# A graph network's adjacency stages: the gathered rows are weighed by ScalarE, tile by tile, in place of VectorE

## The reference, cut to what matters

```
h   = typed_linear(feat[src], W, etype)              # a message per edge
att = sigmoid(leaky_relu(h_l + h_r)) * edge_weight[:, None]
msg = h3.transpose(0, 2, 1) * att[:, None, :]
agg = segment_sum(msg, dst, num_segments=n_nodes)    # edges are sorted by dst
```

## Time and profile before

| | |
|---|---|
| device time, 3 runs | 4801.52 us median (4799.81 to 4803.82) |
| profiled execution | 4794.28 us, span 4792.6 us |
| busy: PE, DVE, ACT, POOL | 3187.0, 3208.5, 1384.8, 3339.1 us |
| mean granted PE clock | 0.827 |
| first stage, first to last gather | 197.8 to 2202.4 us |
| second stage, first to last gather | 2314.8 to 3304.0 us |

### The profile page before, as it was taken

How to read it: one execution, slowest core, us unless ns; L and a number is a source line. 1 busy time by engine, 2 the same in 40 slices (tenths; PEclk the granted TensorE clock), 3 DMA queues, 4 the chain that set the end, 5 groups by cost and what they waited for, 6 DMA issues and landing times. The chain is left out here.

```text
span 4792.6 us, 63834 instructions
## 1 busy us (share of the span) xinstructions
PE 3187.0 (66%) x16141; PEld 1906.6 (40%) x16141; DVE 3208.5 (67%) x5876; ACT 1384.8 (29%) x2465; POOL 3339.1 (70%) x3216
## 2 busy tenths in 40 slices
PE   2667777777777777775555555554678767487795
PEld 2344445445545544543343444443323232222222
DVE  4676776767776677775555555554588777487686
ACT  2422232323232323233322122222233222132352
POOL 0277777777777777773577777775777777777573
PEclk6798888988888898887777777776688879688897
DMA  1233332323332333232222222223356545255583
GB/s 52 98 94 93 94 98 85 102 85 100 92 99 89 96 94 96 90 98 85 91 80 71 65 78 71 71 71 102 89 157 172 149 120 153 75 166 155 159 245 108
DMA packets 355069, 502.09 MB, mean 105 GB/s; under 512 B 92892, under 2 KB 214749, under 8 KB 354574
## 3 DMA queue, kind: packets, MB, share of 16 engines
q1 hardware_dynamic: 251453, 394.51, 25.4%
q0 software_dynamic: 100352, 102.96, 10.1%
q10 hardware_dynamic: 2896, 0.59, 0.1%
HBM read 290.63 MB, written 207.16 MB: 104 GB/s over the span
## 5 line engine op out<-in xcount | busy, mean ns | idle before, releaser
L809 POOL DMA_INDIRECT frows<-messages,fidx x2352 | 2277.5, 968 | 848.5 <-issue 669.3
L889 PE MATMUL fps_b<-hot_key,hot_lo 128*128 128x343 f32 x3136 | 1233.8, 502 | 407.1 <-PEq L70 403.3
L948 DVE TENSOR_TENSOR strip<-strip,fps_b 128x343 f32 x1568 | 787.0, 502 | 541.7 <-DVEq L70 516.5
L1091 POOL DMA_INDIRECT lrows<-messages,lidx x784 | 879.2, 1121 | 271.2 <-issue 223.7
L879 PE MATMUL fps_sum<-hot,frows 128*64 128x80 f32 x4704 | 551.1, 301 | 601.9 <-PEq L70 601.9
L824 ACT ACTIVATE turned<-fps_t 128x512 f32<-128x512 f32 (+1 forms) x754 | 431.6, 572 | 1741.2 <-ACTq L70 1738.8
L889 PEld LDWEIGHTS fps_b<-hot_key,hot_lo 128*128 128x128 f32 x3136 | 541.6, 206 | 728.8 <-issue 679.1
L879 PEld LDWEIGHTS fps_sum<-hot,frows 128*64 128x64 f32 x4704 | 521.9, 194 | 693.0 <-issue 693.0
L918 DVE TENSOR_SCALAR hot_key<-iota_f,edge 128x343 f32<-128x343 f32 x1574 | 750.9, 477 | 0.1
L1236 ACT ACTIVATE pos<-l_c,coeff 128x896 f32<-128x896 f32 x392 | 394.6, 1007 | 725.2 <-PE l_c L1140 725.2
L1140 PE MATMUL l_c<-unit_t,unit_g 64*128 64x448 f32 x1568 | 460.9, 667 | 148.5 <-DVE acc L1278 89.1
(11 more groups left out here) (186 smaller groups left out, 1741.7 us busy)
## 6 DMA issues: line engine op xcount, KB each, us to landing
adj<-turned SPq DMA_DIRECT2D x696, 256.0 KB
edge<-adj SPq DMA_DIRECT2D x294, 448.0 KB
adj_x<-adj SPq DMA_DIRECT2D x98, 448.0 KB
frows<-messages,fidx POOLq DMA_INDIRECT x2352, 2.4
messages<-msg SPq DMA_DIRECT2D x14, 1120.0 KB, 4.6
lrows<-messages,lidx POOLq DMA_INDIRECT x784
adj<-turned SPq DMA_DIRECT2D x58, 64.0 KB
wh_g<-wh_rows SPq DMA_DIRECT2D x56, 32.0 KB, 1.7
```

The source lines that it names most:

```text
L809: pool.indirect_dma_start(rows[:, q, k, :], None, tab_l[l].ap(), bass.IndirectOffsetOnAxis(ap=idx[:, q, k:k + 1], axis=0)).then_inc(s_got[ ...
L889: pe.matmul(ps_b[n % KB][:, 0:NT * TWIN], hot_lo[:, s % 2, k, :], hot_key[:, n % KB, :], start=True, stop=True).then_inc(s_b, 1)
L948: dve.tensor_tensor(part, part, ps_b[n % KB][:, 0:NT * TWIN].rearrange("p (h w) -> p h w", w=TWIN), ALU.add).then_inc(v, 1)
L1091: pool.indirect_dma_start(rows[:, q, k, :], None, tab_l[1].ap(), bass.IndirectOffsetOnAxis(ap=idx[:, q, k:k + 1], axis=0)).then_inc(s_got[ ...
```

## The change

DVE's weighing instruction goes. ACT now waits for the landing itself, copies the indices for row `u + 4`, and weighs row `u` with 14 activations of 128x64, each with a scale per partition read from `edge`. The semaphore `s_idx_free` goes with it. ACT's pieces are no longer taken in a block ahead of a sept's rows: each stands at the tile where PE turns it. Since DVE's order no longer keeps row `u` from being summed before `ps_sum` is read, a new semaphore `s_sum_free` does: DVE raises it when the addition to `feat` is over, and PE takes it ahead of `sum_row`.

```diff
@@ ScalarE
-                    def pieces(k, u):
-                        for piece in PER[u]:
+                    def keep(k, piece):
...
                     with act.Fori(0, LOOPS) as i:
                         for s in range(sept_it):
-                            pieces(1 - s // SPG % 2, s % SPG)
+                            todo = list(PER[s % SPG])
                             for n in range(s * HT, (s + 1) * HT):
+                                if todo and (n % HT % 2 == 1 or n % HT == HT - 1):
+                                    keep(1 - s // SPG % 2, todo.pop(0))
                                 if n in ends:
                                     u = ends[n]
-                                    take(act, s_idx_free[u % RB])
+                                    act.wait_ge(s_got[u % RB], i * (rows_it // RB * JT * 16) + (u // RB + 1) * JT * 16)
                                     indices(u, i * rows_it + (u + RB))
+                                    for k in range(JT):
+                                        last = act.activation(rows[:, u % RB, k, :], rows[:, u % RB, k, :], ACT.Copy, scale=edge[:, A_W, bass.ds((i * rows_it + u) * JT + k, 1)])
+                                    last.then_inc(s_wm, 1)
@@ TensorE, sum_row
                         take(pe, s_wm)
+                        take(pe, s_sum_free)
@@ VectorE, add_sums
                         dve.sem_inc(s_rows_free[u % RB], 1)
-                        take(dve, v_agg)
                         part = feat[:, bass.ds(windows[u], WIN)]
                         dve.tensor_tensor(part, part, ps_sum[0:F, 0:WIN], ALU.add).then_inc(v_agg, 1)
+                        take(dve, v_agg)
+                        dve.sem_inc(s_sum_free, 1)
@@ VectorE, the loop
-                                if n in ends:
-                                    u = ends[n]
-                                    dve.wait_ge(s_got[u % RB], i * (rows_it // RB * JT * 16) + (u // RB + 1) * JT * 16).then_inc(s_idx_free[u % RB], 1)
-                                    dve.tensor_tensor(rows[:, u % RB, :, :], rows[:, u % RB, :, :], per_edge(A_W, (i * rows_it + u) * JT, JT, F), ALU.mult).then_inc(s_wm, 1)
```

More of the change, by code:

```diff
@@ L785, in fs @@
                     return sem(f"f{l}_{name}")
-                s_idx, s_idx_free, s_rows_free = ([fs(f"{n}{q}") for q in range(RB)] for n in ("idx", "idx_free", "rows_free"))
+                s_idx, s_rows_free = ([fs(f"{n}{q}") for q in range(RB)] for n in ("idx", "rows_free"))
                 s_got = [sem(f"f{l}_got{q}", True) for q in range(RB)]
@@ L790, in fast_path @@
                 s_t, s_t_free, s_piece = (fs(n) for n in ("t", "t_free", "piece"))
-                v, v_agg, s_zc, s_iota = fs("v"), fs("v_agg"), fs("zc"), fs("iota")
+                v, v_agg, s_zc, s_iota, s_sum_free = fs("v"), fs("v_agg"), fs("zc"), fs("iota"), fs("sum_free")
                 PIECES = [list(range(k, min(k + 4, NT))) for k in range(0, NT, 4)]
@@ L815, in zero @@
                         return act.activation(part, zcol[:, 0:1].rearrange("p (a b) -> p a b", a=1).to_broadcast([P, n, STRIP]), ACT.Copy)
-                    def pieces(k, u):
-                        for piece in PER[u]:
[L820 to L825, removed]
+                    def keep(k, piece):
+                        a, b = piece[0], piece[-1] + 1
+                        j = side(k, piece)
+                        take(act, s_t)
+                        take(act, s_stored[j], 16)
+                        act.activation(turned[j][:, 0:(b - a) * P], ps_t[j][:, 0:(b - a) * P], ACT.Copy).then_inc(s_t_free, 1)
+                        zero(strip[k][:, a:b, :], b - a).then_inc(s_piece, 1)
                     def indices(u, row):
@@ L838, in _ @@
                         for s in range(sept_it):
-                            pieces(1 - s // SPG % 2, s % SPG)
+                            todo = list(PER[s % SPG])
                             for n in range(s * HT, (s + 1) * HT):
+                                if todo and (n % HT % 2 == 1 or n % HT == HT - 1):
+                                    keep(1 - s // SPG % 2, todo.pop(0))
                                 if n in ends:
                                     u = ends[n]
-                                    take(act, s_idx_free[u % RB])
+                                    act.wait_ge(s_got[u % RB], i * (rows_it // RB * JT * 16) + (u // RB + 1) * JT * 16)
                                     indices(u, i * rows_it + (u + RB))
+                                    for k in range(JT):
+                                        last = act.activation(rows[:, u % RB, k, :], rows[:, u % RB, k, :], ACT.Copy, scale=edge[:, A_W, bass.ds((i * rows_it + u) * JT + k, 1)])
+                                    last.then_inc(s_wm, 1)
                     for u in range(4):
-                        pieces(1, u)
+                        for piece in PER[u]:
+                            keep(1, piece)
                     for j in range(2):
```

## The result

The change makes the kernel slower: 5094.89 us in the median of four runs (5090.95 to 5103.02) against 4802.67 for the kernel before (4799.81 to 4812.78), a ratio of 1.0607 [1.0586, 1.0627]. I had given 4880. The direction came out as forecast. The size did not, +292 where I had +82, and half of the loss comes from a wait that I had put at nothing.

The account below looks back on a forecast made before the run. POOL's gathers bound the kernel; the change would make DVE and PE pace the first stage. +81.2 there, +5.0 at stage ends, -3.7 in the second stage gave +82.5 us on 4794.3, stated as 4880; range 4772 to 4945.

Parts of the forecast that it names:

- heavy case: First stage: PE's clock low at six delayed sums and DVE's addition wait showing, or activations at 0.34 us; 4935 to 4978; chance 0.18.
- own pace: First stage: DVE and PE, left to themselves, go from 278.6 to 298.0 us per round, over POOL's 282.8.
- six four-piece rows: Rows ending at k = 6 with four pieces: weighing ends 3.4 us later, PE waits, 20.4 us per round.
- two one-piece rows: Rows ending at k = 6 with one piece: ACT long free, weighed before PE arrives, -1.4 us each, -2.8 per round.
- eight rows at k = 2: Rows of a round ending at k = 2: the last piece is older, so the delay was taken as 0.
- the clock: PE's `sum_row`: a longer wait ahead invites half clock, 3.96 against 2.12 us; 0 to 11 us per round, taken as 1.8.
- the slack: First stage: DVE's 54.5 us of waiting for landings, 7.8 us per round, taken off 286.4 to give 278.6.
- The activations and their place: ACT: 14 activations at 0.24 us start to start, 3.46 us per row, beginning only after the last piece is kept.
- POOL's relief: Gathers beginning inside a DVE weighing are no longer held up: 24.9 us in the first stage, 3.7 in the second.
- first rival: POOL stays the bound and is relieved, PE and DVE's pace staying under 282.8 us per round: -23.6 us, 4778; chance 0.17.
- POOL's waiting between rows: First stage: POOL, held up by `s_rows_free`, waits between rows, 7 rounds x 15 us = 105 us.

Follow-up runs that it names:

- the later sum: The change with PE's sum and DVE's addition five tiles later in the first stage, three in the second: 4781.64 us, ratio 0.9947 against the kernel before.

## Why the prediction was right in its direction and wrong in its size

Up to the second stage's first gather I had +81.2 and +2.5 for the stage end, so 83.7 us; it was 300.4. The missing 216.7 us divide at the kernel without the wait: 149.1 are the wait, 67.6 the rest. (The split is that of this kernel; with one activation per row the wait costs nothing to be seen.)

**`s_sum_free`: the step that failed.** "DVE waits for its own addition of 0.2 us; taken as nothing, 16 x 0.3 = 4.8 us per round as the upper end." It was 21.3 us per round. I priced the wait by what is waited for, 0.2 us, and not by what stands behind it in DVE's program. The next instruction starts 0.62 us later where it is the strip, and 1.4 us later in the mean where the TENSOR_LOAD of 1.04 us stands behind the wait, which takes away the load's cover. Three runs agree: 144 us back without the wait, 110 lost by it alone on the kernel before, 131 back when it moves one tile. The heavy case that I had at 0.18 named this wait too, with 4.8 us. The Trainium skill, Runtime: NRT & Kernel Launch, "Instruction fetch mechanics", puts a TENSOR_LOAD at some 200 ns per register, as a round trip; it speaks of loads from HBM, and these come from SBUF. An estimate by that page is 1.4 us for 7 offsets. The trace has 1.04, or 149 ns each, and 0.46 for one register alone, so it is lower for seven and higher for one. The load's own record in the trace of before (1.16 us in the median), which I had not looked at, would have been warning enough.

**The own pace without the wait.** I had 298.0 us per round; the kernel without the wait comes to 67.6/7 = 9.7 us more. PE's account of that trace against the one before shows where (first stage, us per round):

| term | forecast | trace |
|---|---|---|
| PE's wait ahead of the sums, six four-piece rows | +20.4 | +19.6 (1.91 to 5.18 us each) |
| the same, two one-piece rows | -2.8 | -5.2 (2.61 to 0) |
| the same, eight rows at k = 2 | 0 | -1.6 (2.53 to 2.33) |
| length of the sums (the clock) | +1.8 | +6.4 (346.2 to 391.3 us in all) |
| sum | +19.4 | +19.2 |

The two sums agree by luck: the clock's term was too small, and those of the one-piece and the k = 2 rows were too high. *The clock* is my heavy case: of the 42 four-piece rows' sums, 4 took over 3 us before and all 42 do now, while in the one-piece rows it went from 12 of 14 to none. What failed beside it is *the slack*. I added the terms to 278.6, the round less DVE's 7.8 us of waiting for landings; they came on top of 286.4. These 7.8, and 2.0 that stand in other waits and products of PE, less the 0.2 between the sums of the table, are the 9.7 within 0.1. The kernel before with the wait alone says the same: DVE's waiting for landings was gone, and yet the stage lost 114 us, where the wait took 118 at its two places. This is read from the traces; no run set the clock or the slack apart.

**The activations and their place.** 335 ns, 14 in 3.44 us, PE's wait of 4.62: all as in the prediction. The place behind the piece costs 109 us by the run that swaps them, with the slow sums that come with it. The lateness of six rows was the right step, with 20.4 us per round.

**POOL's relief.** 24.9 us in the first stage: it was had, POOL's gathers are busy 27.5 us less in the change. In the time it shows only where POOL is the bound, 22 us up to the second stage with one activation. In the change no gather is at 1.66 any more; the longest is 1.16:

```profile
L809 POOL DMA_INDIRECT frows<-messages,fidx x2352: 938/945/1164, 199.1 to 3601.5; - x196
```

The Trainium skill's rule in SBUF — State Buffer, "Who interferes with whom", agrees on this: a two-input VectorE instruction holds up a GpSimd one that reads SBUF, and ScalarE doesn't. The row of 1.66 us and the runs without that weighing say the same. As a forecast for the time the rule alone would have had the wrong sign. That gain is the first rival of the prediction, not the second as it says there. Rival one, 4778, is the case in which the sum has slack: 4768 with one activation, 4782 with the later sum. Two slips of the sum change little: it turns at delays of 0.9 us each with the clock's 1.8 kept in (1.2 is without it), and 4876.8 with the 7 us added is 4884.

**POOL's waiting between rows.** Forecast 105 us; it is 371.9 less the first 67.6, so 304. It follows the pace. The second stage kept its slack: 986.0 us, as forecast within 5 of 989.

Open is what holds up the remaining gathers. In the kernel before, 377 gathers that begin inside a `hot_key` take 19.0 us more than 944 ns each; the 1110 that begin outside both `hot_key` and a weighing take 2.9 us more. I read that from the trace; no run took `hot_key` off DVE.

## What to carry to other kernels

Price a new wait by what stands behind it in the waiting engine's program, above all a register load or another instruction that used to run ahead under queued work. If the wait is needed, put it a tile of work later: that gave back 131 of 144 us here. Don't take an engine's waiting for slack before a run has shown it. Moving work from a bound engine to an idle one pays only if its consumer has slack: count what the idle engine has ahead of it, and move the consumer back by a few tiles in the same change. Here that turns +6% into -0.5%. Then measure the moved consumer on the kernel before as well: it gives -0.3% there without the change.

## What the runs showed of the hardware that I had not expected

- A wait of DVE for its own 0.22 us addition, directly behind it, takes the next instruction from 0.15 to 0.77 us behind the addition's start where no load follows (49 places). Ahead of a load of seven registers (1.04 us) it takes it from 0.16 to 1.99 us in the pair shown. Round ends left out, 42 of 56 such distances were under 0.3 us before; with the wait all 56 are over 1.2.
- A later matrix product's clock is part of a stall's price: sums above 3 us went from 63 to 96 of 112, and the granted clock of the stage from 0.87 to 0.83. The length of the wait ahead of the sum doesn't decide it alone: with 3.43 us in the mean 11 of 42 sums are slow (the weighing ahead of the piece), with 2.36 us 54 of 56 (the rows at k = 2 in the change).
- A gather that begins inside a two-input VectorE instruction ends 0.82 us after it, in 63 of the 69 that begin more than 0.13 us before its end in the kernel before, and in 31 of 34 with the later sum. So it loses most where it begins early: 81 of them cost 24.9 us in one kernel, 86 of them 8.4 us in another with the same instructions.
